# Moving the softmax scale's diagonal from VectorE to GpSimd, and a shorter maximum for one-chunk tiles, in an eight-core post-norm transformer layer

## The chip, the cores and the metric

The kernel runs on all 8 cores of one Trainium2 chip, each core on one sequence of the batch, with the same program and no traffic between the cores. The metric is the device time in microseconds of the slowest core. Each core has a tensor engine (PE, with its weight loads shown as PEld), VectorE (DVE), ScalarE (ACT), GpSimd (POOL) and SyncE (SP); each engine takes its instructions in the order of its own queue, and they meet through semaphores.

## The reference

Per sequence (S = 2048 tokens, D = 2048, 16 query heads of 128, one shared key and value head):

```python
q = (x @ q_w.T + q_b).reshape(b, s, H, HEAD_DIM)
k = x @ k_w.T + k_b
v = x @ v_w.T + v_b
scores = einsum('bqhd,bkd->bhqk', q, k) / HEAD_DIM ** 0.5
scores = where(causal, -inf, scores)
attn = softmax(scores)
out = einsum('bhqk,bkd->bqhd', attn, v).reshape(b, s, H * HEAD_DIM)
x = layernorm(x + out @ o_w.T + o_b)
x = layernorm(x + x @ (weight * scale_weight[:, None]).T + bias)
```

## The kernel before

The program is one long list of operations, each with an engine, the events it waits for and a semaphore that it counts up (class Prog). There is one counter per engine ("t" for PE, "v" DVE, "a" ACT, "p" POOL) and some for DMAs. When an engine's instructions are written out, a wait is left out if the same engine has already waited for an equal or higher count of that semaphore; every other one becomes an instruction of its own in the engine's queue, on line 69 of the code.

There are three stages. First K, V and Q are projected (to about 330 us of the span). Then comes attention (about 366 to 1602 us), and last two rounds of output projection, layer norm, second linear layer and layer norm (to the end).

Attention is tiled by query tile: 128 queries of one head are a unit. Four phases, c = 0 to 3, each take 4 query tiles (j = 0 to 3) of all 16 heads, so 64 units a phase and 256 in all. A unit of phase c looks at (4c + j + 1) x 128 keys, in nkc = c + 1 chunks of up to 512. Within a phase the loop runs over `step` (head, plus two for the drain), and over j, and issues three things in this order:

- `tr_unit(step - 1, c, j)`: the exponentials of the head before are multiplied by a diagonal matrix that holds 1/denominator (diagP), which transposes and scales them at once (PE, line 440). Each group of up to four 128x128 results fills one PSUM bank and is evacuated to expST by DVE (line 459) and ACT (line 464) in turn.
- `av_unit(step - 2, c, j)`, for j <= c: four matmuls with V into psO (PE, line 482) of the head before that; in c = 0 all of a head's are at j = 0. The first waits for all evacuations of that head and for ACT's copy of the psO before (line 491).
- `sc_mms(step, c, j)` and `sc_soft(step, c, j)`: the scores (PE, line 348, and the causal mask with line 357), then the softmax. DVE takes the maximum of each chunk into mpart (line 376), then the negated maximum over the chunks into negm (line 380). ACT takes exp with the sum as a second result (line 397; its ACTIVATION_READ_ACCUMULATOR follows). With more than one chunk DVE adds the sums (den, line 409). DVE takes the reciprocal (rcp, line 414) and multiplies the identity by it to give diagP (line 418), which the PE uses one head later.

Score chunks and transpose groups share a ring of 7 PSUM banks (four in psS, psT0, psT1, psU) in the order of issue: a bank is free again when ACT's exponential or the evacuation of it is done. A unit of phase c takes 2(c + 1) banks.

negm8, den8, rcp8 and diagP have a place for each j and for heads of even and odd number (par); so what a unit writes was last used two heads before, and the waits for E_comb2, E_diag2v, E_dsum2 and E_trmm2 are for that.

POOL issues DMAs for weights in the first stage, then the memsets of the parts of expST that stay zero (line 502: 12 of 128x128 for each phase, all of them to be had once the Q projection is done), and has nothing else until the third stage.

Of the kernel before, what the change touches and what calls it, by code (L numbers as in the profile page):

```python
# [12 lines left out]
AX = mybir.AxisListType  # L13
# [64 lines left out]
def build_program(serial=False):  # L78
# [25 lines left out]
    p = Prog(serial=serial)  # L104
# [4 lines left out]
    with st:  # L109
# [41 lines left out]
        with nc.sbuf_tensor("QTO", [128, NT * S], BF16) as QTO:  # L151
# [17 lines left out]
            with stA:  # L169
# [78 lines left out]
                for ot in range(NT):  # L248
# [4 lines left out]
                        waits=wq, inc="qw%d" % (ot % 2))  # L253
# [49 lines left out]
            negm8 = stB2.enter_context(nc.sbuf_tensor("negm8", [128, 8], F32))  # L303
            den8 = stB2.enter_context(nc.sbuf_tensor("den8", [128, 8], F32))
            rcp8 = stB2.enter_context(nc.sbuf_tensor("rcp8", [128, 8], F32))
            mpart = stB2.enter_context(nc.sbuf_tensor("mpart", [128, 32], F32))
# [14 lines left out]
            E_comb2 = [[None] * 4, [None] * 4]  # L321
            E_dsum2 = [[None] * 4, [None] * 4]
            E_expl2 = [[None] * 4, [None] * 4]
            E_exall2 = [[[] for _ in range(4)], [[] for _ in range(4)]]
            E_diag2v = [[None] * 4, [None] * 4]
            E_trmm2 = [[None] * 4, [None] * 4]
# [39 lines left out]
            def sc_soft(h, c, j, chunks):  # L366
                par = h % 2
                qt = 4 * c + j
                kext = (qt + 1) * 128
                nkc = (kext + W - 1) // W  # L370
                mcol = par * 16 + j * 4
                ncol = par * 4 + j
                mx_all = []
                for s, slot, wdt, kc, E_mm in chunks:
                    mx_all.append(p.op("vector", lambda e, slot=slot, wdt=wdt,
                                mc=mcol + kc: e.reduce_max(  # L376
                        mpart[:, mc:mc + 1], slot[:, 0:wdt], axis=AX.X),
                        waits=[E_mm, E_comb2[par][j]], inc="v"))
                E_comb2[par][j] = p.op("vector", lambda e, mcol=mcol,
                                       nkc=nkc, ncol=ncol: e.reduce_max(  # L380
                    negm8[:, ncol:ncol + 1], mpart[:, mcol:mcol + nkc],
                    axis=AX.X, negate=True),
                    waits=mx_all + E_exall2[par][j], inc="v")
                E_ex = None
                ex_all = []
                for s, slot, wdt, kc, E_mm in chunks:
                    if nkc == 1:
                        acc = den8[:, ncol:ncol + 1]
                        wx = [E_comb2[par][j], E_trmm2[par][j],
                              E_diag2v[par][j]]  # L390
                    else:
                        acc = dpart[:, mcol + kc:mcol + kc + 1]
                        wx = [E_comb2[par][j], E_trmm2[par][j],
                              E_dsum2[par][j]]
                    E_ex = p.op("scalar", lambda e, slot=slot, wdt=wdt,
                                kc=kc, ncol=ncol, acc=acc, par=par, qt=qt:
                                e.activation(  # L397
                        expS8[:, (par * 4 + qt % 4) * S + kc * W:
                              (par * 4 + qt % 4) * S + kc * W + wdt],
                        slot[:, 0:wdt], AF.Exp,  # L400
                        bias=negm8[:, ncol:ncol + 1], scale=1.0,
                        accum_out=acc), waits=wx, inc="a")
                    ring_free.append((s, E_ex))
                    ex_all.append(E_ex)
                E_expl2[par][j] = E_ex
                E_exall2[par][j] = list(ex_all)
                if nkc > 1:
                    E_dsum2[par][j] = p.op("vector", lambda e, mcol=mcol,
                                           nkc=nkc, ncol=ncol: e.reduce_sum(  # L409
                        den8[:, ncol:ncol + 1], dpart[:, mcol:mcol + nkc],  # L410
                        axis=AX.X),
                        waits=ex_all + [E_diag2v[par][j]], inc="v")
                E_den = E_dsum2[par][j] if nkc > 1 else E_expl2[par][j]
                E_rq = p.op("vector", lambda e, ncol=ncol: e.reciprocal(
                    rcp8[:, ncol:ncol + 1], den8[:, ncol:ncol + 1]),
                    waits=[E_den, E_diag2v[par][j]], inc="v")
                E_diag2v[par][j] = p.op("vector", lambda e, par=par, j=j,
                                        ncol=ncol: e.tensor_scalar(  # L418
                    diagP[:, (par * 4 + j) * 128:(par * 4 + j + 1) * 128],
                    ident_s[:], rcp8[:, ncol:ncol + 1], None,  # L420
                    AluOpType.mult),
                    waits=[E_rq, E_trmm2[par][j]], inc="v")

            def tr_unit(h, c, j):
                par = h % 2
# [70 lines left out]
            for c in range(NCH):  # L496
                for sl in range(2):
                    ev = None
                    for kt in range(4 * c + 1, 4 * c + 4):
                        for jj in range(kt - 4 * c):  # L500
                            ev = p.op("gpsimd", lambda e, sl=sl, kt=kt,
                                      jj=jj: e.memset(
                                expST2[:, sl * NT * W + kt * W + jj * 128:
                                       sl * NT * W + kt * W +
                                       (jj + 1) * 128], 0.0),
                                waits=[E_Q_all], inc="p")
                    E_msd[sl] = ev
                for step in range(H + 2):
                    for j in range(4):
                        if 1 <= step <= H:  # L510
                            tr_unit(step - 1, c, j)
                        if step >= 2 and j <= c:
                            av_unit(step - 2, c, j)
                        if step < H:
                            sc_soft(step, c, j, sc_mms(step, c, j))
# [5 lines left out]
            for ot in range(2):  # L521
# [3 lines left out]
                    waits=[E_Q_all, E_wob], inc="wo%d" % (ot % 2))  # L525
            xT4 = xT_h.rearrange("(t p) s -> t p s", p=128)
            for ot in range(3):
# [3 lines left out]
                    waits=[E_Q_all], inc="xr%d" % (ot % 3))  # L531
# [491 lines left out]
```

How the kernel before makes its waits and increments, by code:

```python
    def emit(self, eng_name, eng, sems):  # L62
        hi = {}
        for idx, (name, fn, waits, inc) in enumerate(self.ops):
            if name != eng_name:
                continue
            for s, v in waits:
                if hi.get(s, 0) < v:
                    eng.wait_ge(sems[s], v)
                    hi[s] = v
            ins = fn(eng)
            if inc is not None:
                if ins is None:
                    ins = eng.nop()
                ins.then_inc(sems[inc], SEMS[inc])
# [2 lines left out]
def build_program(serial=False):  # L78
# [870 lines left out]
                        pend[k]()  # L949
                    if pend_end is not None:
                        pend_end()
                    if bi + 1 < len(blocks):
                        preload(*blocks[bi + 1])
                    pend, pend_end = make_tail(kind, c)
                for k in range(len(pend)):
                    pend[k]()
                p.op("gpsimd", lambda e: (
                    e.wait_ge(sems["od0"], 16 * odc[0]),
                    e.wait_ge(sems["od1"], 16 * odc[1]),
                    e.wait_ge(sems["od2"], 16 * odc[2]))[-1])
```

## Time and profile before

| | before |
|---|---|
| median of three runs | 2408.8 us (2404.6 to 2446.0) |
| the profiled execution | 2401.9 us, of which the span of its slowest core 2400.4 us |
| spans of the 8 cores | 2382.0 to 2400.4 us |
| busy: PE, DVE, ACT, POOL | 1560.0, 956.0, 841.0, 334.5 us |
| mean granted TensorE clock, slowest core | 0.78 of full speed |

All times below are of the profiled execution, on its slowest core (core 3), in us from the start of its span. Busy time says how long an engine worked, not whether anything waited for it; a row of the timeline is start, length and what was done, with the idle time before it and what ended that in brackets. A releaser is inferred by the profile, so where the engine named had long been done, or the code has no such wait, it was another.

### The profile page before, as it was taken

Reading aid. Unit: us, or ns where it says so; the run is one execution under the profiler, and the core shown is the slowest. Engines: PE = TensorE matmul, PEld = TensorE weight load, DVE = VectorE, ACT = ScalarE, POOL = GpSimd, SP = SyncE. Lnnn points to the kernel's source line nnn. Section 1 sums busy time; section 2 is a strip of 40 time slices with the busy share of each in tenths; the row PEclk is TensorE's granted clock in tenths of the full one; section 3 lists DMA queues with packets and bytes.
Section 4 is the critical chain, followed back from the end, with each engine's and each line's share of the span. In section 5 each row is a group of like instructions: output and inputs, shape, how many; then the busy total and the mean of one; then the engine's idle time right before and its main releaser. Section 6 shows DMA issues by size and latency. Waiting matters only on the chain.

```text
span 2400.4 us, 25983 instructions; the slowest of 8 cores (2382.0 to 2400.4 us)
## 1 busy us (share of the span) xinstructions
PE 1560.0 (65%) x7216; PEld 671.1 (28%) x7216; DVE 956.0 (40%) x2241; ACT 841.0 (35%) x2078; POOL 334.5 (14%) x335
## 2 busy tenths in 40 slices
PE   0799944445546566666565566668759686786873
PEld 0344412222223222222222223333223232232321
DVE  0000004545555555555555555540416414044334
ACT  0112103444444445444444454442233321223421
POOL 0000010000000000000000000004435343344431
PEclk9999975666566677666577776679889898898986
DMA  9222299600000000000000000005433345452242
GB/s 142 35 44 35 37 119 108 80 1 1 1 1 1 1 1 1 1 1 1 1 1 1 1 1 1 1 23 157 129 113 114 109 141 162 137 167 75 93 154 96
DMA packets 43639, 137.06 MB, mean 57 GB/s; under 512 B 5835, under 2 KB 5868, under 8 KB 42988
## 3 DMA queue, kind: packets, MB, share of 16 engines
q0 software_dynamic: 5296, 34.60, 11.1%
q1 hardware_dynamic: 28988, 84.02, 10.9%
q10 hardware_dynamic: 9216, 16.78, 2.8%
q8 instruction: 63, 1.03, 0.2%
q14 instruction: 76, 0.62, 0.1%
HBM read 153.21 MB, written 33.55 MB: 78 GB/s over the span
## 4 chain that ended last, share of the span: by engine, by line
PE 36%; DVE 18%; issue 16%; DMA 12%; ACT 10%; another core or an unknown queue 3%; POOL 3%; DVEq 1%; ACTq 0%; SPq 0%; POOLq 0%
PE psT L259 9%; ACT expS L397 8%; DVE mpart L376 8%; DMA xres<-xT 7%; PE psO L482 6%; PE psT L834 4%; DVE expST L459 3%; POOL ycs L795 3%; PE psS L348 2%; DMA outT<-outb 2%; PE psU L834 2%; PE psO L834 2%; DMA trib_s<-tri 2%; PE psS L440 2%
## 5 line engine op out<-in xcount | busy, mean ns | idle before, releaser
L397 ACT ACTIVATE expS<-psS,negm 128x512 bf16<-128x512 f32 (+3 forms) x367 | 225.0, 620 | 402.0 <-DVE negm L380 402.0
L376 DVE TENSOR_REDUCE mpart<-psS 128x1 f32<-128x512 f32 (+3 forms) x367 | 205.7, 597 | 368.3 <-PE psS L357 364.8
L482 PE MATMUL psO<-expST,Vsb 128*128 128x512 bf16 x640 | 261.9, 556 | 94.4 <-DVE diagP L418 57.8
L795 POOL TENSOR_TENSOR ycs<-yscr,xres 128x512 f32<-128x512 f32 x64 | 84.3, 1318 | 1495.1 <-ACT yscr L784 1331.9
L440 PE MATMUL psS<-diagP,expS 128*128 128x128 bf16 x1250 | 153.4, 264 | 153.2 <-ACT expS L397 117.4
L259 PE MATMUL psT<-xTbf,qwst 128*128 128x512 bf16 x1024 | 221.2, 379 | 0.2 <-ACT Vsb L241 0.2
L348 PE MATMUL psS<-KT,QTO 128*128 128x512 bf16 (+3 forms) x367 | 162.5, 479 | 79.0 <-ACT expS L397 45.5
L409 DVE TENSOR_REDUCE den<-dpart 128x1 f32<-128x2 f32 (+2 forms) x192 | 29.9, 156 | 418.1 <-ACT expS L397 402.1
L397 ACT ACTIVATE expS<-psT,negm 128x512 bf16<-128x512 f32 (+3 forms) x179 | 110.8, 624 | 189.8 <-DVE negm L380 189.8
L636 DVE TENSOR_SCALAR rowb<-psS 1x512 f32<-1x512 f32 x8 | 5.4, 681 | 400.3 <-PE psS L616 400.3
L440 PEld LDWEIGHTS psS<-diagP,expS 128*128 128x128 bf16 x1250 | 104.6, 118 | 202.2 <-issue 196.0
L834 PE MATMUL psT<-x1T,fwst 128*128 128x512 bf16 x512 | 125.9, 403 | 38.2 <-ACT x1T L718 29.2
L440 PE MATMUL psT<-diagP,expS 128*128 128x128 bf16 x632 | 80.5, 265 | 86.7 <-ACT expS L397 69.1
L259 PEld LDWEIGHTS psT<-xTbf,qwst 128*128 128x128 bf16 x1024 | 100.1, 98 | 120.9 <-issue 0.4
L768 PE MATMUL psT<-QTO,wost 128*128 128x512 bf16 x512 | 121.9, 394 | 11.3 <-DMA wost<-wo_bf 10.1
L482 PEld LDWEIGHTS psO<-expST,Vsb 128*128 128x128 bf16 x640 | 73.4, 127 | 177.2 <-issue 164.4
L808 ACT CAST castsc<-ycs 128x512 bf16<-128x512 f32 x64 | 39.6, 619 | 233.6 <-POOL ycs L795 233.6
L858 POOL TENSOR_TENSOR ycs<-zscr,ycs 128x512 f32<-128x512 f32 x64 | 86.8, 1357 | 194.0 <-ACT zscr L850 194.0
L459 DVE CAST expST<-psS 128x512 bf16<-128x512 f32 (+2 forms) x183 | 113.1, 631 | 1.1 <-PE psS L440 0.7
L348 PE MATMUL psT<-KT,QTO 128*128 128x512 bf16 (+3 forms) x179 | 84.8, 501 | 40.0 <-ACT expS L397 21.8
L273 ACT ACTIVATE QTO<-psT,qbs_s 128x512 bf16<-128x512 f32 x64 | 44.0, 687 | 177.5 <-PE psT L259 177.5
L376 DVE TENSOR_REDUCE mpart<-psT 128x1 f32<-128x512 f32 (+3 forms) x179 | 103.3, 601 | 3.6 <-PE psT L348 3.6
(91 smaller groups left out, 2282.9 us busy)
## 6 DMA issues: line engine op xcount, KB each, us to landing
wost<-wo_bf SPq DMA_DIRECT2D x64, 512.0 KB, 4.2
fwst<-fw_bf SPq DMA_DIRECT2D x64, 512.0 KB, 3.3
xres<-xT ACTq DMA_DIRECT2D x64, 256.0 KB, 4.1
outT<-outb SPq DMA_DIRECT2D x64, 256.0 KB, 3.1
xTbf<-xT POOLq DMA_DIRECT2D x1, 8192.0 KB, 64.8
qwst<-qw POOLq DMA_DIRECT2D x16, 512.0 KB, 5.5
wo_bf<-wo POOLq DMA_DIRECT2D x4, 2048.0 KB, 80.0
fw_bf<-fw POOLq DMA_DIRECT2D x4, 2048.0 KB, 98.5
```

The lines of the kernel that those rows point to most:

```text
L259: e.matmul(bk[:], qwst[:, (ot % 2) * D + dt * 128: (ot % 2) * D + dt * 128 + 128], xTbf[:, dt * S + c * W: dt * S + c * W + W], start=(dt ...
L273: e.activation(QTO[:, ot * S + c * W: ot * S + c * W + W], bk[:], AF.Identity, bias=qbs_s[:, ot:ot + 1], scale=INV_SQRT_DK),
L348: wdt=wdt, dgc=diag_chunk: e.matmul(slot[:, 0:wdt], QTO[:, h * S + qt * 128: h * S + qt * 128 + 128], KT[:, kc * W: kc * W + wdt], start=T ...
L376: mc=mcol + kc: e.reduce_max(mpart[:, mc:mc + 1], slot[:, 0:wdt], axis=AX.X),
L397: e.activation(expS8[:, (par * 4 + qt % 4) * S + kc * W: (par * 4 + qt % 4) * S + kc * W + wdt], slot[:, 0:wdt], AF.Exp, bias=negm8[:, nco ...
L440: qt=qt: e.matmul(bk[:, i * 128:(i + 1) * 128], expS8[:, (par * 4 + qt % 4) * S + kt * 128: (par * 4 + qt % 4) * S + (kt + 1) * 128], diag ...
L459: e.tensor_copy(d, s), waits=[last_mm],
L482: base=base: e.matmul(bk[:, 0:W], Vsb[:, kt * 128:(kt + 1) * 128], expST2[:, base + kt * W: base + (kt + 1) * W], start=(kt == 0), stop=(k ...
L768: ot=ot: e.matmul(bk[:], wost[:, (ot % 2) * D + ht * 128: (ot % 2) * D + ht * 128 + 128], QTO[:, ht * S + c * W: ht * S + c * W + W], star ...
L795: pbuf=pbuf: e.tensor_tensor(pbuf[:, ot * W:(ot + 1) * W], yscr[:, (ot % 2) * W:(ot % 2) * W + W], xres[:, (ot % 3) * W:(ot % 3) * W + W], ...
L834: ot=ot: e.matmul(bk[:], fwst[:, (ot % 2) * D + dt * 128: (ot % 2) * D + dt * 128 + 128], x1T[:, dt * W:(dt + 1) * W], start=(dt == 0), st ...
L858: pbuf=pbuf: e.tensor_tensor(pbuf[:, ot * W:(ot + 1) * W], zscr[:, (ot % 2) * W:(ot % 2) * W + W], pbuf[:, ot * W:(ot + 1) * W], AluOpType ...
```

## The change

It has two parts, both in `sc_soft`. Where a unit has one chunk (phase c = 0, 64 units) the maximum of the chunk is no longer written to mpart and reduced a second time; one reduce_max with negate writes negm directly, with the waits of both. And the multiplication that makes diagP (256 units) is issued to GpSimd and counts its semaphore "p" instead of DVE's "v". All that waited for the diag (PE's transposes, den or the reciprocal two heads later, the exponential in c = 0) waits for POOL's count from now on.

```diff
--- before.py
+++ after.py
@@ -370,17 +370,26 @@
                 nkc = (kext + W - 1) // W
                 mcol = par * 16 + j * 4
                 ncol = par * 4 + j
-                mx_all = []
-                for s, slot, wdt, kc, E_mm in chunks:
-                    mx_all.append(p.op("vector", lambda e, slot=slot, wdt=wdt,
-                                mc=mcol + kc: e.reduce_max(
-                        mpart[:, mc:mc + 1], slot[:, 0:wdt], axis=AX.X),
-                        waits=[E_mm, E_comb2[par][j]], inc="v"))
-                E_comb2[par][j] = p.op("vector", lambda e, mcol=mcol,
-                                       nkc=nkc, ncol=ncol: e.reduce_max(
-                    negm8[:, ncol:ncol + 1], mpart[:, mcol:mcol + nkc],
-                    axis=AX.X, negate=True),
-                    waits=mx_all + E_exall2[par][j], inc="v")
+                if nkc == 1:
+                    _s, slot1, wdt1, _kc, E_mm1 = chunks[0]
+                    E_comb2[par][j] = p.op("vector", lambda e, slot=slot1,
+                                           wdt=wdt1, ncol=ncol: e.reduce_max(
+                        negm8[:, ncol:ncol + 1], slot[:, 0:wdt],
+                        axis=AX.X, negate=True),
+                        waits=[E_mm1, E_comb2[par][j]]
+                        + E_exall2[par][j], inc="v")
+                else:
+                    mx_all = []
+                    for s, slot, wdt, kc, E_mm in chunks:
+                        mx_all.append(p.op("vector", lambda e, slot=slot,
+                                    wdt=wdt, mc=mcol + kc: e.reduce_max(
+                            mpart[:, mc:mc + 1], slot[:, 0:wdt], axis=AX.X),
+                            waits=[E_mm, E_comb2[par][j]], inc="v"))
+                    E_comb2[par][j] = p.op("vector", lambda e, mcol=mcol,
+                                           nkc=nkc, ncol=ncol: e.reduce_max(
+                        negm8[:, ncol:ncol + 1], mpart[:, mcol:mcol + nkc],
+                        axis=AX.X, negate=True),
+                        waits=mx_all + E_exall2[par][j], inc="v")
                 E_ex = None
                 ex_all = []
                 for s, slot, wdt, kc, E_mm in chunks:
@@ -414,12 +423,12 @@
                 E_rq = p.op("vector", lambda e, ncol=ncol: e.reciprocal(
                     rcp8[:, ncol:ncol + 1], den8[:, ncol:ncol + 1]),
                     waits=[E_den, E_diag2v[par][j]], inc="v")
-                E_diag2v[par][j] = p.op("vector", lambda e, par=par, j=j,
+                E_diag2v[par][j] = p.op("gpsimd", lambda e, par=par, j=j,
                                         ncol=ncol: e.tensor_scalar(
                     diagP[:, (par * 4 + j) * 128:(par * 4 + j + 1) * 128],
                     ident_s[:], rcp8[:, ncol:ncol + 1], None,
                     AluOpType.mult),
-                    waits=[E_rq, E_trmm2[par][j]], inc="v")
+                    waits=[E_rq, E_trmm2[par][j]], inc="p")
 
             def tr_unit(h, c, j):
                 par = h % 2
```

## Rows read from the trace of the kernel before

**Rows 1.** Windows view, attention: length, PE, PEld, DVE, ACT, POOL busy, PEclk, DMA share, GB/s.

```profile
366.00:1602.00 1236.00, 715.96 (x3648) 335.44 (x3647) 678.05 (x1913) 571.61 (x1656) 0.00 (x0) 0.67 0.08 9
```

**Rows 2.** Waits view, attention stage: us in total, times, longest us.

```profile
DVE den L409 <- ACT expS L397: 402.1, 184, 3.3
...
DVE rcp L414 <- ACT expS L397: 51.5, 63, 1.0
...
DVE mpart L376 <- PE psT L348: 3.6, 1, 3.6
...
ACT expS L397 <- DVE negm L380: 689.8, 256, 40.6
```

**Rows 3.** Timeline of DVE, one unit of c = 2: start us, length us, what.

```profile
1003.46 0.16 DVE L409 TENSOR_REDUCE den<-dpart 128x1 f32<-128x3 f32 x1 [2.27 <-ACT expS L397]
...
1003.72 0.16 DVE L414 RECIPROCAL rcp<-den 128x1 f32<-128x1 f32 x1
...
1003.99 0.26 DVE L418 TENSOR_SCALAR diagP<-ident_s,rcp 128x128 bf16<-128x128 bf16 x1
...
1004.16 0.68 DVE L459 CAST expST<-psS 128x512 bf16<-128x512 f32 x1
```

**Rows 4.** The line of diag: count, duration ns min/median/max, first and last start.

```profile
L418 DVE TENSOR_SCALAR diagP<-ident_s,rcp x256: 253/254/256, 367.5 to 1601.7; 128x128 bf16<-128x128 bf16 x128
```

**Rows 5.** Timeline of PE, DVE and ACT in c = 0, where a head begins.

```profile
484.78 0.58 ACT L464 CAST expST<-psS 128x512 bf16<-128x512 f32 x1
...
484.98 0.16 DVE L414 RECIPROCAL rcp<-den 128x1 f32<-128x1 f32 x1 [0.87 <-ACT expS L397]
...
485.42 0.68 DVE L376 TENSOR_REDUCE mpart<-psS 128x1 f32<-128x512 f32 x1
...
485.50 1.87 PE L482 MATMUL psO<-expST,Vsb 128*128 128x512 bf16 x4 [4.04 <-DVE diagP L418]
...
486.21 0.15 DVE L380 TENSOR_REDUCE negm<-mpart 128x1 f32<-128x1 f32 x1
...
486.46 0.69 ACT L397 ACTIVATE expS<-psS,negm 128x512 bf16<-128x512 f32 x1 [1.10 <-DVE negm L380]
...
487.27 0.31 PE L357 MATMUL psT<-trib_s,ident_s 128*128 128x128 bf16 x1
...
487.35 0.16 DVE L414 RECIPROCAL rcp<-den 128x1 f32<-128x1 f32 x1 [0.98 <-ACT expS L397]
...
487.78 0.28 DVE L459 CAST expST<-psS 128x128 bf16<-128x128 f32 x1
...
487.99 0.28 DVE L376 TENSOR_REDUCE mpart<-psT 128x1 f32<-128x128 f32 x1
```

**Rows 6.** Timeline of POOL and DVE after attention, and the waits (line 69) before 1714.45.

```profile
1712.83 1.27 POOL L795 TENSOR_TENSOR ycs<-yscr,xres 128x512 f32<-128x512 f32 x1 [3.35 <-ACT yscr L784]
...
1712.99 0.69 DVE L687 COPY abc_s<-psS 128x512 f32<-128x512 f32 x1 [5.96 <-PE psS L673]
...
1713.60 0.68 DVE L689 COPY bbc_s<-psS 128x512 f32<-128x512 f32 x1
...
1714.30 1.04 POOL L812 TENSOR_TENSOR castsc<-ycs 128x512 bf16<-128x512 f32 x1 [0.20 <-POOL ycs L795]
...
1714.45 1.43 DVE L701 TENSOR_TENSOR ycs<-ycs,abc_s 128x512 f32<-128x512 f32 x1 [0.17 <-DVE bbc_s L689]
...
L69 DVEq EVENT_SEMAPHORE  x2: 21/21/21, 1714.3 to 1714.4; - x2
```

**Rows 7.** Two lines of POOL: count, duration ns min/median/max.

```profile
L502 POOL MEMSET expST<- x48: 194/194/204, 325.4 to 332.2; 128x128 bf16 x48
...
L812 POOL TENSOR_TENSOR castsc<-ycs x64: 1038/1039/1302, 1619.6 to 2175.9; 128x512 bf16<-128x512 f32 x64
```

**Rows 8.** Timeline in c = 3: first scores of a unit, and its first maxima.

```profile
1418.47 1.06 PE L348 MATMUL psT<-KT,QTO 128*128 128x512 bf16 x2
...
1420.15 1.28 DVE L376 TENSOR_REDUCE mpart<-psT 128x1 f32<-128x512 f32 x2
```

## The prediction

> **What bounds the kernel now.** I read the windows view first. In the attention stage (366 to 1602 us, half the span) the PE is busy 716 of 1236 us, DVE 678, ACT 572 and POOL not at all [rows 1]. No engine is full, but DVE and ACT together give 678 + 572 = 1250 us in 1236: that is what two engines look like when they take turns. The waits view says who waits for whom [rows 2]. DVE stood 402.1 us in front of the sum of the denominators (L409, phases c = 1 to 3) and 51.5 us in front of the reciprocal (L414, phase c = 0), both times for ACT's exponentials. ACT stood 689.8 us, all 256 times, for DVE's negated maximum (L380). DVE waited for the PE only in three single stretches inside the stage (at the start of a phase; the longest is shown, 3.6 us) besides the wait for the stage to begin. So the stage is one closed chain: maxima and negm on DVE, exponentials on ACT, den, rcp and diag on DVE, then the next unit's evacuation casts and maxima. The PE works beside it, some units ahead.
>
> The timeline shows the piece that the change touches [rows 3]: den at 1003.46, rcp at 1003.72, diag at 1003.99, the next cast at 1004.16. All four are in DVE's queue one behind another and nothing fills the gaps: the 0.44 us from rcp's start to the cast's start are chain time, of which the diag's own busy time says little (254 ns, all 256 alike [rows 4]).
>
> **The diag leaves DVE.** Without it the cast follows rcp directly. DVE starts an independent instruction before the last one has quite ended: the 128-wide cast at 487.78 lasts 0.28 and the next starts 0.21 later [rows 5], so behind a 0.16 us rcp the next could start after 0.08 to 0.09 us. Upper bound for the gap: the 0.17 from diag to cast today [rows 3]. I take 0.10, since the cast has no dependence on rcp and its matmuls are long done. Saved per unit: 0.44 - 0.10 = 0.34 us (bounds 0.27 to 0.36).
>
> **A wait comes in its place.** Den (c >= 1) and rcp (c = 0) list the diag of two heads before. That was an older count of DVE's own semaphore and needed no wait of its own; now it is a count of POOL's, always long satisfied, but a wait to be executed behind the wait for ACT, so on the chain. The price: L701 at 1714.45 starts 0.17 us after its producer ended, with two waits in DVE's queue (the row of line 69 counts them) [rows 6]; with one wait it is 0.10 (den ends 1003.62, rcp starts 1003.72 [rows 3]). So one satisfied wait is 0.07 us; the low bound is nothing. Behind it in DVE's queue stand rcp, the casts and all maxima of the next unit, and ACT waits for those. PE's transposes get a POOL wait in exchange for a DVE wait, at no cost on the chain.
>
> Net per unit in c = 1 to 3: 0.34 - 0.07 = 0.27 us; 192 units: 51.8 us.
>
> **Phase c = 0, the shortcut.** With one chunk the maximum goes straight to negm. Today the maximum at 485.42 ends at 486.10, negm starts at 486.21 and the exponential at 486.46; directly it would start 0.10 after the maximum (as it does after negm, 486.36 to 486.46), at 486.20: 0.26 saved [rows 5]. Three new satisfied waits: on rcp (0.07), on the exponential for the old diag (0.07, ACT's price taken like DVE's), and on the maximum for the old negm, which shows only in units with no cast ahead of it, two of four (0.035 on average). Per unit 0.34 + 0.26 - 0.175 = 0.42; four units, one head: 1.70 us.
>
> But here the PE has little in hand once per head. In [rows 5] ACT evacuates the last transposes (484.78 to 485.36), only then can the four psO matmuls run (485.50; the row names the diag as releaser, but by the code they wait for evacuations and the old psO copy, so the cast that ended at 485.36 is what it waited for), and behind them in PE's queue stand the next head's scores, ended at 487.27 + 0.31 = 487.58. DVE could use them at about 487.68; it does at 487.99. Slack: 0.3 us. On the other side, between 484.98 and 487.99, the change takes out two diags and one negm and adds four waits: 0.68 + 0.26 - 0.28 = 0.66 us. So 0.36 of it is lost to a new wait of DVE for the PE. For 14 heads 1.70 - 0.36 = 1.34, for the first two (no psO work yet) 1.70: 22.2 us. Bounds: 27 if the PE is faster there, 17 if the waits cost more.
>
> **What POOL takes over** lies beside the chain. The nearest rows are a 128-wide memset, 0.194 us, and a 512-wide product, 1.04 us [rows 7]; a 128-wide product should be between, say 0.5. The diag of a unit is needed by the PE for transposes that DVE or ACT evacuates three units later, 7 us even in c = 0, where a unit takes 2.37 us (484.98 to 487.35 [rows 5]); even 1.04 is covered. The 12 memsets of each later phase now wait in POOL's queue behind the diags of the phase before: about 2.4 us, at a time when only transposes and psO work are left and no diag is due. If that cover were gone it would cost those 2.4 us three times.
>
> **Does the PE hold in c = 3?** There each unit has 8 banks' worth of work for a ring of 7, so the PE can't run far ahead. In [rows 8] the first two score matmuls of a unit are both done at 1418.47 + 1.06 = 1419.53, and their maxima start at 1420.15 and, one 0.60 us step on, at 1420.75: at least 0.62 us in hand for the first and 1.22 for the second. The change uses 0.27. It holds.
>
> **DVE against POOL.** The likely objection is that the two get in each other's way. At 1712.83 to 1714.10 POOL adds, and DVE's copy from PSUM at 1712.99 lies wholly inside; it takes 0.69 us, and the one at 1713.60, partly inside, 0.68. At 1714.30 POOL starts again and DVE's L701, with two SBUF inputs, takes 1.43 [rows 6]. So the clash is real, but for instructions with two SBUF inputs; the casts and maxima of the attention stage read one PSUM operand, like the copies. I cost it at nothing; the high end is below, among the rivals.
> The Trainium skill has a rule against such a change, in Perfetto Trace Analysis, section Optimizing Scalar/DVE Operations: the two engines share a read port, so moving work between them "might not help". Its page SBUF — State Buffer, section Who interferes with whom, limits this to DVE instructions with two SBUF inputs or in a two-port mode; the trace agrees with the second (0.69 against 1.43). By the first alone the sum would be near nothing, by the second it stands.
>
> **Sum.** 51.8 + 22.2 - 1 (the last diag of each phase is not on the chain: the PE ends a phase) = 73 us. The stages before and after are untouched. From the profiled execution's 2401.9 us: 2329. The other runs shown lie 3 to 7 us above it, so I say 2332. As the smallest change that a measurement of this kernel can tell is about 2% (48 us), 73 us is just clearly visible.
>
> **Rivals.**
> - Contention (slower). If the instruction behind each rcp were stretched as L701 is, by 1.43 - 0.69 = 0.74 us, a unit would lose 0.74 - 0.27 instead of gaining 0.27: 256 x 0.47 = 120 us slower, 2522. It turns from gain to loss where POOL stops DVE for more than 0.27 us a unit. For: POOL will always run right behind rcp. Against: the PSUM copies above. This is the skill's rule taken at its word. Chance 0.06.
> - The PE takes the place of the diag (no change). Were there a PE wait that I don't see, so that in c = 3 and c = 2 nothing is gained, 128 x 0.27 = 35 us fall away: 2367. For: the PE is busy 58% at a reduced clock and has only 0.6 us in hand. Against: DVE hardly ever waits for it. Chance 0.06.
> - POOL too slow (no change or slower). If a diag took over 2 us, POOL would set the pace in c = 0; at 2.5 us, 64 x (2.5 - 2.37) + the lost 22 = 30 us: 2362. Against: four 128-wide parts of a 512-wide product take 1.04 us in all. Chance 0.02.
> - More than forecast: waits at no cost (256 x 0.07 = 18 us), the shortest issue gap (5 us) and no PE wait in c = 0 (5 us): 2304. This is the low end of my own forecast, not a case of its own.
>
> **How the numbers follow.** My forecast has 0.86. Its own range: 2304 below; above, a gap of 0.17 in place of 0.10 (256 x 0.07 = 18 us) and 5 us in c = 0 give 2355, and 5 more for the scatter of the runs 2360. The rivals outside it hold 0.14, so 2304 to 2360 stands as the range. Faster by over 2% means below 2361: 0.86. Within 2%: the second and third rival, 0.08. Slower: 0.06.
>
> **What would show it.** Line of diag on POOL, 256 times, 0.2 to 1 us; no DVE instruction of the attention stage longer than before; rcp to next cast about 0.10; two waits before den and 0.07 more between the last exponential and den; c = 0 with DVE waiting about 0.3 us for the PE in each head's first maximum; attention stage shorter by some 73 us, about 17 in each of c = 1, 2 and 3. A c = 3 without its 17 us would prove the PE rival; longer casts the first one.

## The result, and the profile after

| | before | after |
|---|---|---|
| median | 2406.5 us (10 runs) | 2322.4 us (10 runs) |
| ratio, 95% interval | | 0.967 (0.964 to 0.969) |
| profiled execution | 2401.9 us | 2323.0 us |
| first to last rcp (attention), mean of the 8 cores | 1234.2 us | 1156.9 us |
| to the first rcp; from the last rcp to the end, mean | 364.1; 795.1 us | 359.3; 797.4 us |

The change saves 84 us of the median (3.3% by the ratio); 2332 was forecast. 77.3 us of it lie in the attention stage. The other stages differ by -4.8 and +2.3 us between these two executions. They are the same code, and over all the runs below they scatter from 359 to 364 and from 795 to 802 us, so I read nothing into that. In some executions the cores of a die show a lower clock and take longer, and diag_only has only one run without this, scores_first and pool_twice two each, so the tables compare profiled executions, all of them undisturbed.

The phases of attention after the change, by the lines of rcp in four windows (count, duration ns, first and last start; core 7, now the slowest):

```profile
L423 DVE RECIPROCAL rcp<-den x64: 162/164/166, 359.9 to 473.0; 128x1 f32<-128x1 f32 x64
...
L423 DVE RECIPROCAL rcp<-den x64: 162/164/165, 481.0 to 723.6; 128x1 f32<-128x1 f32 x64
...
L423 DVE RECIPROCAL rcp<-den x64: 162/164/165, 732.7 to 1065.3; 128x1 f32<-128x1 f32 x64
...
L423 DVE RECIPROCAL rcp<-den x64: 162/164/165, 1078.9 to 1517.3; 128x1 f32<-128x1 f32 x64
```

As means of the eight cores, first to last rcp of a phase:

| phase | before | after | saved | by the prediction's terms |
|---|---|---|---|---|
| c = 0 | 137.8 | 113.6 | 24.2 | 22.2 |
| c = 1 | 261.3 | 242.6 | 18.7 | 17.3 |
| c = 2 | 349.7 | 332.6 | 17.1 | 17.3 |
| c = 3 | 455.6 | 438.4 | 17.2 | 17.3 |

The last column counts 64 units a phase. From first to last rcp there are 63 turns; for those the terms give 17.0 in c = 1 to 3.

The unit that answers to [rows 3], in DVE's and POOL's timeline:

```profile
1001.15 0.15 DVE L418 TENSOR_REDUCE den<-dpart 128x1 f32<-128x3 f32 x1 [2.38 <-ACT expS L406]
...
1001.41 0.16 DVE L423 RECIPROCAL rcp<-den 128x1 f32<-128x1 f32 x1
1001.51 0.69 DVE L468 CAST expST<-psT 128x512 bf16<-128x512 f32 x1
1001.80 0.60 POOL L427 TENSOR_SCALAR diagP<-ident_s,rcp 128x128 bf16<-128x128 bf16 x1 [4.88 <-PE psT L449]
```

From rcp to the cast it was 0.44 us and is 0.10. Over all units that a cast follows, on all eight cores, the medians are 0.44 and 0.10 as well. POOL starts its diag 0.39 us after rcp started and takes 0.60, beside the cast. The line of the diag on POOL answers to [rows 4]:

```profile
L427 POOL TENSOR_SCALAR diagP<-ident_s,rcp x256: 602/602/607, 360.2 to 1517.7; 128x128 bf16<-128x128 bf16 x128
```

The waits view of the stage has kept the shape of [rows 2]: DVE waits for ACT and ACT for DVE. New is a wait of DVE for the PE in c = 0 (us in total, times, longest us; first DVE's rows, then ACT's):

```profile
DVE den L418 <- ACT expS L406: 393.4, 173, 3.1
DVE rcp L423 <- ACT expS L406: 59.6, 64, 1.3
...
DVE negm L376 <- PE psU L357: 1.5, 3, 0.6
DVE negm L376 <- PE psS L357: 1.1, 3, 0.4
DVE negm L376 <- PE psT L357: 1.0, 3, 0.4
```

```profile
ACT expS L406 <- DVE negm L389: 520.3, 192, 3.9
ACT expS L406 <- DVE negm L376: 37.4, 45, 1.8
```

### The profile page after: what moved, and what is told of

Its sections match the earlier page's. It is cut to its first block, busy times and chain, and to the rows that moved or that the text cites. A ratio compares the mean times of both kernels' runs of the same rounds, so it can differ in the third digit from the quotient of the medians.

```text
span 2321.4 us, 26657 instructions; the slowest of 8 cores (2305.4 to 2321.4 us)
## 1 busy us (share of the span) xinstructions
PE 1551.8 (67%) x7216; PEld 670.7 (29%) x7216; DVE 890.4 (38%) x1921; ACT 840.6 (36%) x2078; POOL 489.0 (21%) x591
## 4 chain that ended last, share of the span: by engine, by line
PE 38%; issue 16%; DVE 16%; DMA 13%; ACT 10%; POOL 3%; another core or an unknown queue 3%; DVEq 1%; ACTq 0%; SPq 0%; POOLq 0%
PE psT L259 10%; ACT expS L406 8%; DVE mpart L385 8%; DMA xres<-xT 8%; PE psO L491 6%; PE psT L843 5%; DMA outT<-outb 3%; POOL ycs L804 3%; PE psS L348 3%; PE psU L843 2%; PE psO L843 2%; PE psS L449 2%; DVE expST L468 2%; DMA trib_s<-tri 2%
## 5 line engine op out<-in xcount | busy, mean ns | idle before, releaser
L427 POOL TENSOR_SCALAR diagP<-ident_s,rcp 128x128 bf16<-128x128 bf16 x256 | 154.2, 602 | 1036.8 <-DVE rcp L423 711.5
L491 PE MATMUL psO<-expST,Vsb 128*128 128x512 bf16 x640 | 255.0, 543 | 69.1 <-ACT expST L473 42.5
L385 DVE TENSOR_REDUCE mpart<-psS 128x1 f32<-128x512 f32 (+3 forms) x329 | 187.4, 610 | 3.6 <-PE psS L348 3.6
L376 DVE TENSOR_REDUCE negm<-psS 128x1 f32<-128x256 f32 (+3 forms) x38 | 18.5, 488 | 358.9 <-PE psS L357 358.8
```

Of the source, the lines that this page charges most:

```text
L385: wdt=wdt, mc=mcol + kc: e.reduce_max(mpart[:, mc:mc + 1], slot[:, 0:wdt], axis=AX.X),
L427: ncol=ncol: e.tensor_scalar(diagP[:, (par * 4 + j) * 128:(par * 4 + j + 1) * 128], ident_s[:], rcp8[:, ncol:ncol + 1], None, AluOpType.mult),
L491: base=base: e.matmul(bk[:, 0:W], Vsb[:, kt * 128:(kt + 1) * 128], expST2[:, base + kt * W: base + (kt + 1) * W], start=(kt == 0), stop=(k ...
```

## The experiments

Attention is given as first to last rcp, mean of the 8 cores, with its four phases (the rest of the stage lies between them).

| kernel | profiled, us | attention | c = 0 | c = 1 | c = 2 | c = 3 |
|---|---|---|---|---|---|---|
| before | 2401.9 | 1234.2 | 137.8 | 261.3 | 349.7 | 455.6 |
| short_only | 2389.3 | 1217.8 | 121.2 | 261.4 | 349.8 | 455.7 |
| diag_only | 2335.7 | 1170.0 | 125.9 | 243.0 | 332.3 | 438.7 |
| after | 2323.0 | 1156.9 | 113.6 | 242.6 | 332.6 | 438.4 |
| wait_early | 2312.8 | 1141.7 | 108.9 | 238.4 | 329.5 | 434.3 |
| scores_first | 2325.4 | 1154.6 | 111.0 | 242.6 | 332.6 | 438.5 |
| pool_twice | 2326.9 | 1158.9 | 114.1 | 242.6 | 332.7 | 438.5 |
| pool_four | 2403.2 | 1232.5 | 176.9 | 242.6 | 332.6 | 438.4 |
| defer_pool | 1983.7 | 816.6 | 81.2 | 160.5 | 212.4 | 333.4 |
| defer_dve | 2016.1 | 839.6 | 85.3 | 169.7 | 223.0 | 332.8 |
| defer_early | 1988.5 | 816.7 | 79.6 | 160.6 | 211.3 | 335.6 |
| defer_scores | 1934.5 | 770.2 | 76.4 | 146.7 | 210.8 | 305.9 |

**The two parts alone.** diag_only is the kernel before with the second hunk of the diff, short_only the changed kernel with the second hunk taken back:

```diff
-                E_diag2v[par][j] = p.op("gpsimd", lambda e, par=par, j=j,
+                E_diag2v[par][j] = p.op("vector", lambda e, par=par, j=j,
...
-                    waits=[E_rq, E_trmm2[par][j]], inc="p")
+                    waits=[E_rq, E_trmm2[par][j]], inc="v")
```

> Only the second part of the change: the diag on POOL, the two-step maximum kept. By the prediction's terms: c = 1 to 3 gain 0.27 us a unit (0.34 for the diag, less 0.07 for the satisfied wait on POOL), 52 us in all; c = 0 gains 0.34 - 0.07 - 0.07 = 0.20 a unit, 13 us, of which some 2 are lost to the PE once per head. Sum 62 us, plus up to 5 us for the fewer issue stalls seen after the change: 2340 to 2345 against 2406. Rival (the shortcut matters for more than its one instruction, or the two parts need each other): less than 50 us.

> Only the first part of the change: one reduce_max per unit in c = 0, the diag stays on DVE. By the terms: 0.26 us for each of 64 units = 17 us, no new wait on the chain, and the one maximum that could meet the PE (the first of a head) has 0.3 us in hand for 0.26 used. So 2389 against 2406, and c = 1 to 3 as before. Rival (the PE already sets the pace of c = 0 at the head's first unit): a third of it less, 11 us.

Measured on the stage: diag_only -64.2 us (62, and up to 5 more, were expected), short_only -16.4 (17 expected; ratio of the whole 0.994, 0.990 to 0.999, a change under 2%). diag_only as a whole took 2335.7 us where 2340 to 2345 was expected. Each phase moves only where its part says so. The two alone make 80.6; together they save 77.3, 3.3 less. The loss is in c = 0: 11.9 and 16.6 make 28.5, both together 24.2. The 2 us that diag_only should have lost to the PE were not seen: its DVE has no wait for the PE in c = 0 besides the opening one.

**The PE in c = 0.** scores_first changes the order in PE's queue, for c = 0 alone:

```diff
+                        ch = None
+                        if step < H and c == 0:
+                            ch = sc_mms(step, c, j)
                         if step >= 2 and j <= c:
                             av_unit(step - 2, c, j)
                         if step < H:
-                            sc_soft(step, c, j, sc_mms(step, c, j))
+                            sc_soft(step, c, j, ch or sc_mms(step, c, j))
```

> The changed kernel, with the scores of a head's first unit put ahead of the psO matmuls of two heads before in PE's queue, in c = 0 only. If the PE takes back some 4 us of c = 0 (the first maximum of a head waits for scores queued behind the psO work), c = 0 shrinks from 113.6 us (first to last reciprocal) to about 109 and the first maxima no longer wait for the PE; the rest as it is: 2318. Rival (the 4 us by which the two parts of the change fall short of their sum have another cause): no change in c = 0.

c = 0 went from 113.6 to 111.0, where about 109 was expected, and in c = 0 no maximum waits for the PE's masked scores any more beyond the opening wait. In the total this can't be told from the changed kernel (2324.8 us, the median of two runs, against 2322.4). So the PE took 2.6 us of the missing 4.3, not all. The other part has a likely cause that no run isolates: only with both parts in does a maximum in c = 0 need its own wait for the old negm, since with the diag or the second reduction on DVE a later count of the same semaphore had already been waited for. If, as the prediction has it, two units of four show it, that is 32 x 0.07 = 2.2 us.

**The satisfied wait.** wait_early keeps every dependence and moves the place where it is waited for:

```diff
                             mpart[:, mc:mc + 1], slot[:, 0:wdt], axis=AX.X),
-                            waits=[E_mm, E_comb2[par][j]], inc="v"))
+                            waits=[E_mm, E_comb2[par][j],
+                                   E_diag2v[par][j]], inc="v"))
...
                         wx = [E_comb2[par][j], E_trmm2[par][j],
-                              E_diag2v[par][j]]
+                              E_rq2[par][j]]
```

(The single maximum of c = 0 gets E_diag2v too; E_rq2 holds the event of the reciprocal of two heads before, whose reading of den8 is what the exponential really has to follow.)

> The changed kernel, with the satisfied wait on POOL's diag moved from den (c = 1 to 3) and rcp (c = 0) to the unit's maxima, where DVE's queue can work it off while a cast still runs, and the exponential's wait in c = 0 put on the old reciprocal, which needs no wait of its own. If a satisfied wait on the chain costs 0.07 us: 192 x 0.07 = 13 us, and 3 to 7 us in c = 0 (one wait of ACT, half of DVE's, part of it taken back by the PE): 16 to 20 us faster than the changed kernel, about 2304. The gap from ACT's accumulator read to den goes from 0.17 back to 0.10. Rival (satisfied waits cost nothing there and the 0.07 is something else): no difference, 2322.

Measured: 15.2 us off the stage, 4.7, 4.2, 3.1 and 4.1 by phase, where 0.07 x 64 = 4.5 was expected of each of the last three. That is a little under the 16 to 20 expected. The whole moved less, to a median of 2315.0 us where 2304 was expected; ratio to before 0.961 (0.959 to 0.964), against 0.967 (0.964 to 0.969) of the changed kernel. So the wait's price is read from the stage, not from the total. In the timeline of wait_early, ACT's accumulator read and DVE's den behind it:

```profile
999.42 0.21 ACT L408 ACTIVATION_READ_ACCUMULATOR expS<-psS,negm 128x1 f32 x1
...
999.72 0.16 DVE L420 TENSOR_REDUCE den<-dpart 128x1 f32<-128x3 f32 x1 [1.99 <-ACT expS L408]
```

and in that of the changed kernel:

```profile
1000.77 0.21 ACT L406 ACTIVATION_READ_ACCUMULATOR expS<-psT,negm 128x1 f32 x1
...
1001.15 0.15 DVE L418 TENSOR_REDUCE den<-dpart 128x1 f32<-128x3 f32 x1 [2.38 <-ACT expS L406]
```

From the read's end to den it is 999.63 to 999.72, 0.09 us, with the wait moved, and 1000.98 to 1001.15, 0.17 us, with it on the chain. Over all units of the eight cores the medians are 0.10 us before the change, 0.17 after it and 0.10 in wait_early. The wait had long been satisfied by its count; here it costs DVE its own 0.07 us each time that DVE stands idle before it.

**What POOL's time costs.** pool_twice and pool_four put the same multiplication into POOL's queue two and four times, each waiting for the one before:

```diff
+                E_d1 = p.op("gpsimd", lambda e, par=par, j=j,
+                            ncol=ncol: e.tensor_scalar(
+                    diagP[:, (par * 4 + j) * 128:(par * 4 + j + 1) * 128],
+                    ident_s[:], rcp8[:, ncol:ncol + 1], None,
+                    AluOpType.mult),
+                    waits=[E_rq, E_trmm2[par][j]], inc="p")
...
-                    waits=[E_rq, E_trmm2[par][j]], inc="p")
+                    waits=[E_d1], inc="p")
```

> The changed kernel with every diag made twice on POOL, one after the other, so that POOL works about 1.3 us a unit in place of 0.6. Cover theory: the diag has a whole head of time and DVE's casts and maxima don't share a port with it, so nothing changes, 2322 within 3 us; one unit takes 1.8 us in c = 0, more than 1.3. Contention rival: DVE's instructions that run beside the second diag get longer, and the kernel loses up to 0.6 us x 256 = 150 us; any lengthening of the 0.68 us casts would show it.

> The changed kernel with every diag made four times on POOL, one after the other: 4 x 0.6 us and three waits of 0.1 to 0.2, about 2.8 us a unit. Cover theory: POOL now sets the pace where a unit takes less than that, in c = 0 (1.8 us): 63 x (2.8 - 1.8) = 63 us slower there, and nothing in c = 1 (3.85 us a unit), 2 and 3. So 2385 against 2322 of the changed kernel. Contention rival: c = 1 to 3 grow too, since POOL runs beside nearly every DVE instruction there.

Twice: the stage is 2.0 us longer, no phase by more than 0.5; the whole took 2326.9 and 2333.2 us, a little outside the 3 us allowed (ratio 0.968, 0.966 to 0.971; the changed kernel has 0.967). Four times: c = 1, 2 and 3 stay at the changed kernel's 242.6, 332.6 and 438.4 us, and c = 0 grows from 113.6 to 176.9, by 63.3 us where 63 was expected. The stage grows by 75.6 us in all. The other 12 lie between the phases: 7.5 between c = 0 and c = 1, where the PE's last transposes wait for POOL's backlog, then 3.7 and 1.0. These were not foreseen, so the whole missed its forecast of 2385: the profiled execution took 2403.2 us, and with ratio 0.998 (0.994 to 1.002) the kernel is back where it was before the change. In pool_four POOL ran beside 72% of DVE's instructions in the stage, and DVE's maxima kept their length:

```profile
L385 DVE TENSOR_REDUCE mpart<-psT x161: 281/681/692, 554.8 to 1574.0; 128x1 f32<-128x512 f32 x122, 128x1 f32<-128x256 f32 x15, 128x1 f32<-128x384 f32 x12, 128x1 f32<-128x128 f32 x12
```

The 512-wide casts are a hair longer: they average 683 ns in short_only (diag on DVE), 688 in the changed kernel and 689 in pool_twice and pool_four. But this is not POOL's doing. Taken apart by the instruction in front of them, on all eight cores, only the casts right behind a rcp have grown: 692 ns, against 683 behind the diag before, and maxima right behind a rcp take 692 too. Casts behind another cast take 680 ns before and after, and 681 in pool_four with POOL at work beside them. And 692 is also what a cast takes in the kernel before, with POOL idle, where DVE stood idle ahead of it (691 to 692, 24 casts). So what counts is what stands ahead in DVE's queue. The next instruction starts 0.608 us after such a cast in place of 0.601, so this costs the chain 0.007 us a unit.

```profile
L468 DVE CAST expST<-psT 128x512 bf16<-128x512 f32 x60 | 41.0, 683 | 0.2 <-PE psS L348 0.2
```

```profile
L468 DVE CAST expST<-psT 128x512 bf16<-128x512 f32 x62 | 42.7, 688 | 0.0
```

(The groups by line and form, 600 to 1500 us: short_only, then the changed kernel; the number behind the busy time is the mean in ns.)

**Opening the chain.** If DVE and ACT take turns, the larger cost may be not what stands in DVE's turn but that there are turns. defer_pool issues den, rcp and diag of a unit one unit later:

```diff
+                pend_soft.append((h, c, j, list(ex_all)))
+
+            def sc_fin(h, c, j, ex_all):
...
                 if nkc > 1:
                     E_dsum2[par][j] = p.op("vector", lambda e, mcol=mcol,
...
+                        old = pend_soft[:]
+                        del pend_soft[:]
                         if step < H:
                             sc_soft(step, c, j, sc_mms(step, c, j))
+                        for u in old:
+                            sc_fin(*u)
```

defer_dve is the same with the diag on DVE.

> The changed kernel with den, rcp and diag of a unit issued one unit later, behind the next unit's casts, maxima and negm. If the stage is one closed chain of DVE and ACT taking turns, this opens it: DVE takes the next maxima while ACT still works on the exponentials, and the unit goes from 1.8, 3.85, 5.3, 7.0 us to about 1.5, 3.0, 4.2, 5.8 (the busy times of DVE, ACT and PE and, in c = 3, the ring of 7 banks): 1157 to about 930 us for the stage, 2095 in all. Rival (the ring closes the chain again, since the next scores need banks that the exponentials free): c = 2 and 3 hardly move, 2250.

> As the run before, but the diag on DVE. In the closed chain its place was worth 0.27 us a unit. In the open one it costs DVE only its 0.17 us of issue distance and a wait, in time that DVE may have: 0 to 0.2 us a unit, so 0 to 50 us slower than with the diag on POOL, most in c = 1 and 2 where DVE and ACT are the fullest. If it were again the full 70 us or more, the chain would not be open.

defer_pool: 1985.5 us median, ratio 0.822 (0.816 to 0.827), 340 us off the stage where 227 were expected. Its timeline shows the turns gone: the maxima at 696.71 and 699.84 now run beside exponentials of the unit before (ACT at 696.57 and 699.49), and den comes behind negm, for exponentials that are long done.

```profile
696.57 0.47 ACT L408 ACTIVATE expS<-psS,negm 128x256 bf16<-128x256 f32 x1
696.71 0.68 DVE L387 TENSOR_REDUCE mpart<-psU 128x1 f32<-128x512 f32 x1
...
697.01 0.59 ACT L482 CAST expST<-psT 128x512 bf16<-128x512 f32 x1
697.31 1.15 DVE L387 TENSOR_REDUCE mpart<-psS 128x1 f32<-128x512 f32 x2
698.56 0.16 DVE L391 TENSOR_REDUCE negm<-mpart 128x1 f32<-128x3 f32 x1
698.82 0.69 ACT L408 ACTIVATE expS<-psU,negm 128x512 bf16<-128x512 f32 x1 [0.72 <-DVE negm L391]
698.88 0.15 DVE L427 TENSOR_REDUCE den<-dpart 128x1 f32<-128x3 f32 x1 [0.15 <-issue]
...
699.49 0.68 ACT L408 ACTIVATE expS<-psS,negm 128x512 bf16<-128x512 f32 x1
...
699.84 0.68 DVE L387 TENSOR_REDUCE mpart<-psT 128x1 f32<-128x512 f32 x1
```

With the diag on DVE the stage is 23.0 us longer (4.1, 9.2, 10.6 and -0.6 by phase), inside the 0 to 50 expected: on the open chain the same instruction is worth about a third of what it was on the closed one (64.2, diag_only), and in c = 3 nothing.

**What holds the open chain.** Two further versions: defer_early is defer_pool with wait_early's edits, and defer_scores also puts the scores ahead of psO in all phases:

```diff
+                        ch = sc_mms(step, c, j) if step < H else None
                         if step >= 2 and j <= c:
                             av_unit(step - 2, c, j)
...
-                            sc_soft(step, c, j, sc_mms(step, c, j))
+                            sc_soft(step, c, j, ch)
```

> The deferred kernel (diag on POOL) with the satisfied waits moved to the maxima as in wait_early. There the move was worth 15 us of the stage, 0.06 us a unit, because the wait stood on the closed chain. In the open one den, rcp and their waits are often worked off while ACT or the PE holds the unit up: 0 to 10 us, 1980 against 1985. If it is again 15 us or more, DVE sets the pace by itself.

> As defer_early, and in all phases the scores of a unit are put ahead of the psO matmuls in PE's queue. In the deferred kernel DVE's maxima waited some 90 us in all for the PE, most for scores queued behind four psO matmuls. If the PE's order is what holds them, these waits mostly go and the stage shrinks by 20 to 50 us, to about 780. Rival (in c = 2 and 3 the scores wait for banks that the exponentials free, and psO then stands idle behind them): c = 3 grows, and the sum is nothing or a loss.

Moving the waits, worth 15 us on the closed chain, gives nothing here (816.7 against 816.6; 0 to 10 expected). Moving the scores gives 46.5 us, inside the 20 to 50 expected: 1937.8 us median, ratio 0.804 (0.802 to 0.806), the fastest of all. The fear for c = 3 did not come true: it gains the most, 29.7 us, and c = 2 almost nothing (0.5). The windows view over the stage, first the changed kernel, then defer_scores (length; PE, PEld, DVE, ACT, POOL busy; granted clock, DMA share, GB/s):

```profile
359.00:1518.00 1159.00, 706.34 (x3649) 335.26 (x3646) 613.97 (x1593) 571.53 (x1657) 159.10 (x292) 0.69 0.08 10
```

```profile
360.00:1130.00 770.00, 555.04 (x3627) 301.03 (x3626) 620.00 (x1587) 566.63 (x1646) 158.19 (x290) 0.85 0.13 16
```

DVE's 614 and ACT's 572 us, which added up to the 1159 of the stage and 2% more, are now 620 and 567 in 770: DVE is busy 81% of the stage.

## Why the prediction was right

**The closed chain** was the step that carried the rest, and it holds. Changes of less than half a microsecond in DVE's turn came out nearly in full in every phase, though no engine was busy for more than 61% of the stage; and defer_pool, which changes no work but only the order of three small instructions, took 340 us off, part of it through a higher granted clock of the PE (last section).

**The diag, 0.34 us a unit.** The rcp to cast distance went from 0.44 to 0.10, the value taken between 0.08 and 0.17. The 0.007 us that the cast behind it gives back was not in the sum, and the sign "no DVE instruction of the attention stage longer than before" did not quite hold: that cast takes 692 ns for 683.

**The wait, 0.07 us a unit.** The least certain term, since it rested on one place in another stage [rows 6]. The distance from the accumulator read to den went from 0.10 to 0.17, and wait_early gave 4.2, 3.1 and 4.1 us for 4.5 in c = 1 to 3. By the median turn, which leaves single long turns out, it is 4.3, 4.3 and 4.2. Without this term the prediction would have said 18 us more. Net, c = 2 and 3 came out at 17.1 and 17.2 of 17.3 us.

**Phase c = 0: 24.2 for 22.2.** short_only gave 16.4 for the 16.6 of the direct maximum. The PE did come up as the new wait, at the place named in [rows 5]; the timeline of the changed kernel at the start of a head shows it:

```profile
458.57 0.31 PE L357 MATMUL psT<-trib_s,ident_s 128*128 128x128 bf16 x1
...
459.06 0.29 DVE L376 TENSOR_REDUCE negm<-psT 128x1 f32<-128x128 f32 x1 [0.34 <-PE psT L357]
```

But this term was sized too large. The profile has nine such waits of 0.4 us where 14 were counted on, and taking them away gave 2.6 us, not 5 (14 x 0.36). My slack of 0.3 us came from one head and left the other heads' out.

**What was moved to POOL** cost nothing that shows, as said, at 0.60 us where 0.5 was guessed. The rival of a slow POOL was put at the right place, c = 0, but sized too small. It set POOL's time against 2.37 us a unit, read from one stretch of [rows 5] that holds the start of a head; the mean turn of c = 0 was 137.8 / 63 = 2.19 us, and 1.80 after the change. For the 2.8 us of pool_four its sum gives 64 x (2.8 - 2.37) = 28 us in c = 0 above the kernel before; measured were 39.1, and the 12 us between the phases come on top.

**Contention** was judged unlikely from the copies in [rows 6] and is ruled out by pool_four, in which c = 1 to 3 did not grow at all. The Trainium skill's rule in SBUF — State Buffer (section Who interferes with whom), that a DVE instruction with at most one SBUF input and outside the two-port modes does not contend, agrees with the trace: casts behind a cast took 681 ns in pool_four, with POOL beside them, and 681 in short_only, without POOL. The Trainium skill's caution in Perfetto Trace Analysis (section Optimizing Scalar/DVE Operations), that moving work between the two engines "might not help", would have misled here: the move was worth 64.2 us.

**The boundary term** (-1 us) came true. The turn of a phase's last unit lies outside the 63 of the table, and the stretches between the phases stayed at 29.8 us before and 29.7 after, so nothing was gained there. With 63 turns a phase the terms give the 73 us of the sum.

**Where luck helped.** The stage gained 77.3 us, 4 more than 73. The median turn of c = 1 to 3 (all eight cores, each place j apart, from rcp to rcp) is 0.262 to 0.265 us shorter, except at the one place of c = 1 where every second turn before held a stall (last section). That is 0.34 - 0.07 - 0.007, and 63 such turns make 16.6 us. The other 2.1, 0.5 and 0.6 us of c = 1, 2 and 3 come from single turns that were longer before, at least in c = 1 by the stalls, which the prediction did not know of. So c = 2 and 3 met their 17.3 so closely in part by luck: a small cost that was left out and these turns nearly cancel. The 7 us between the stage's 77 and the median's 84 are within what the other stages scatter.

## What to carry to other kernels

Where the busy times of two engines add up to the stage and each waits almost only for the other, count the distance from start to start of the instructions in a turn, waits included, not their busy time, and take out of the turn whatever the next turn doesn't need. Better still, look for the instruction that closes the loop: here den and rcp stood ahead of the next unit's maxima, and issuing them one unit later was worth four times as much as the whole change. A dependence moved to another engine can bring a wait of its own, and where that wait stands decides its price: 0.07 us each time on the closed chain here, nearly all of it gone where the wait stood behind a running instruction.

## What the runs showed of the hardware that I had not expected

**Issue stalls.** From the start of the record of a wait in DVE's queue that has been met to the start of the instruction behind it there are usually 0.065 us. At a few places there are 0.35 us more, at nearly the same places on all eight cores. One of them in the kernel before (ACT's accumulator read ends at 572.73, den starts 0.45 later in place of 0.10; the profile names the following cast, which den does not wait for):

```profile
572.53 0.20 ACT L397 ACTIVATION_READ_ACCUMULATOR expS<-psS,negm 128x1 f32 x1
572.62 0.26 ACT L464 CAST expST<-psS 128x128 bf16<-128x128 f32 x1
573.18 0.15 DVE L409 TENSOR_REDUCE den<-dpart 128x1 f32<-128x2 f32 x1 [2.00 <-ACT expST L464]
```

In attention I count 20 of them in DVE's queue before (4, 8, 4, 4 by phase, 6.9 us; 18 to 20 by core) and 6 after (1, 1, 2, 2; 2.2 us). The records of DVE's queue, waits included, show a pattern: every one of these stalls falls on a multiple of 128 records from the others, on all eight cores, before the change and after it. Not every 128th record shows one (in attention there are 36 such places before and 33 after): at some, DVE is still busy with the instruction before, and at others the record is itself a wait, which the count leaves out. With 320 DVE instructions fewer other instructions come to stand on these places. That fits the 1.4 us that c = 1 gained beyond its term and a part of the 4 us that the stage did. What the chip does there no run here settles.

**The PE's clock rose with the shorter stage.** Over the attention stage the granted clock was 0.69 of full speed in the changed kernel and 0.85 in defer_pool and defer_scores, between the levels of 1.2 and 2.4 GHz, with the same matmuls in 71% and two thirds of the time. In defer_pool, four psO matmuls take 1.91 us at 701.93, with a granted clock of 0.50 (1.2 GHz) in that stretch, and 1.03 us at 705.27, with 1.00 (2.4 GHz). Part of the 113 us by which defer_pool beat its forecast is probably this, since the busy times that I had added up were those at the lower clock; it wasn't measured apart.
